# A fused layernorm, filter and FFN kernel: the first tiles centred on VectorE and scaled on ScalarE, the first up blocks by halves of the tokens, and chunk 1's rows loaded and their statistics taken sooner

## The reference, cut to what matters

```python
x = L0_attn_x                        # (2, 4096, 256) float32: 8192 tokens of 256
xn = (x - mean(x)) / sqrt(var(x) + 1e-5)          # over the last axis
# branch 1: a circulant filter whose spectrum hangs on one number D, got by
# counting how many of the first 4, 16, ... 1024 values of xn lie above their mean
x1 = ifft(fft(xn) * filt(D)).real
bits = (sigmoid(x1 @ W_el + b_el) > 0.5)          # 24 a token, then a code word is mended
branch1 = x1 + corrected(bits) @ W_le + b_le
# branch 2: FFN, 256 -> 1024 -> 256
h = gelu(xn @ w1 + b1)
branch2 = h @ w2 + b2
out = x + branch1 + branch2
```

## Time and profile before

| | |
|---|---|
| median of 3 runs | 407.75 us (407.51 to 407.8) |
| the profiled execution | 407.3 us, of which the span of the profile is 405.5 us |
| PE busy | 99% of the span, 1774 matmuls |
| DVE, ACT, POOL busy | 74%, 55%, 21% |

### The profile page before, as it was taken

One profiled execution on the slowest core, in us unless ns is written; L12 is line 12 of the kernel. 1 busy time (PEld: TensorE's weight loads), 2 busy tenths in 40 slices (PEclk: granted clock), 3 DMA queues, 4 the chain that ended last, 5 costly groups with the idle time before them and its releaser, 6 DMA issues.

```text
span 405.5 us, 5548 instructions
## 1 busy us (share of the span) xinstructions
PE 400.7 (99%) x1774; PEld 329.1 (81%) x1774; DVE 298.7 (74%) x512; ACT 223.3 (55%) x333; POOL 87.2 (21%) x102
## 2 busy tenths in 40 slices
PE   8999999999999999999999999999999999999997
PEld 3888888888888888888888888888888888888886
DVE  5879985878658795677957788476974868757656
ACT  3967556557354664537545474554736556365561
POOL 3142421313003131121313013131121312113000
PEclk9999999999999999999999999999999999999999
DMA  6554333213333213333123332023333031111011
GB/s 187 218 158 156 104 103 106 63 42 104 103 104 98 44 65 103 104 103 97 46 64 104 103 104 90 26 91 103 104 103 78 40 89 53 54 52 52 2 52 52
DMA packets 15307, 35.75 MB, mean 88 GB/s; under 512 B 5440, under 2 KB 6592, under 8 KB 15296
## 3 DMA queue, kind: packets, MB, share of 16 engines
q1 hardware_dynamic: 15152, 35.49, 27.4%
q10 hardware_dynamic: 144, 0.13, 0.1%
HBM read 27.17 MB, written 8.45 MB: 88 GB/s over the span
## 4 chain that ended last, share of the span: by engine, by line
PE 97%; DMA 1%; DVE 1%; POOL 0%; SPq 0%; issue 0%
PE p_h L964 43%; PE p_f L982 28%; PE p_f L987 14%; PE p_s L1030 5%; PE p_l L1017 4%; PE p_s L1038 2%; DMA x_sb<-x 1%; PE p_f L997 0%; SPq L248 0%; DVE stats L830 0%; POOL row_nums L361 0%; DVE rows_sb L817 0%; PE p_g L1006 0%; PE p_l L1006 0%; PE p_s L1139 0%
## 5 line engine op out<-in xcount | busy, mean ns | idle before, releaser
L446 ACT ACTIVATE h<-p_h,small_sb 128x512 f32<-128x512 f32 x128 | 88.2, 689 | 139.4 <-PE p_h L964 138.9
L633 DVE TENSOR_TENSOR h_lo<-h,h_hi 128x512 fp32r<-128x512 f32 x128 | 102.9, 804 | 69.2 <-ACT h_hi L454 69.2
L982 PE MATMUL p_f<-h_hi,w_hi 128*128 128x512 f32 x252 | 98.3, 390 | 0.0
L982 PE MATMUL p_f<-h_hi,w_lo 128*128 128x512 f32 x252 | 98.1, 389 | 0.0
L369 POOL TENSOR_TENSOR uv<-xn 128x512 f32<-128x512 f32 x30 | 59.3, 1996 | 126.0 <-DVE xn L618 126.0
L454 ACT CAST h_hi<-h 128x512 fp32r<-128x512 f32 x128 | 79.5, 621 | 5.8
L964 PE MATMUL p_h<-xT_hi,w_hi 128*128 128x512 f32 (+1 forms) x258 | 79.4, 389 | 0.0
L964 PE MATMUL p_h<-xT_lo,w_hi 128*128 128x512 f32 (+1 forms) x258 | 79.2, 388 | 0.0
L964 PE MATMUL p_h<-xT_hi,w_lo 128*128 128x512 f32 (+1 forms) x258 | 79.0, 387 | 0.0
L987 PE MATMUL p_f<-h_lo,w_hi 128*128 128x512 f32 x252 | 77.6, 389 | 0.0
L964 PEld LDWEIGHTS p_h<-xT_lo,w_hi 128*128 128x128 f32 x258 | 48.3, 188 | 10.3 <-DVE xT_lo L839 0.2
(11 more groups left out here) (127 smaller groups left out, 325.2 us busy)
## 6 DMA issues: line engine op xcount, KB each, us to landing
xt_sb<-xt SPq DMA_DIRECT2D x16, 512.0 KB, 5.3
x_sb<-x SPq DMA_DIRECT2D x15, 512.0 KB, 4.6
rows_sb<-rows_dram SPq DMA_DIRECT2D x15, 512.0 KB, 4.4
out<-xt_sb SPq DMA_DIRECT2D x15, 512.0 KB, 2.8
xt_sb<-w SPq DMA_DIRECT2D x3, 512.0 KB, 7.5
xt_sb<-w SPq DMA_DIRECT2D x2, 256.0 KB, 4.5
x_sb<-x SPq DMA_DIRECT2D x2, 128.0 KB, 2.1
x_sb<-x SPq DMA_DIRECT2D x1, 256.0 KB, 3.2
```

The source lines that it names most:

```text
L446: nc.scalar.activation(h[m % 2][:], p_h[:, m % 2, :], ACT.Gelu, bias=small_sb[:, S_B1 + m:S_B1 + m + 1]).then_inc(gelu_done, 1)
L633: nc.vector.tensor_tensor(h_lo[m % HR][:], h[m % 2][:], h_hi[m % HR][:].bitcast(F32), ALU.subtract).then_inc(h_lo_done, 1)
L982: mm(p_f[:, a, :], w[:, m, a * HF:(a + 1) * HF], h_hi[r][:], start=(m == 0 and w is w2_hi), stop=False, skip_group_check=True)
```

## The change

- Chunk 0's first two tiles: DVE subtracts the mean as soon as it is known (`centred0`), ACT multiplies with the inverse deviation (`scaled0`). The other two tiles stay with one DVE instruction each, now behind the first `w1_lo` piece.
- The identity matrix is made on POOL (`affine_select` on the matrix of ones, in front of four memsets) and is no longer loaded.
- `w1`'s first quarter becomes two eighths, in loads and in splitting.
- Up blocks 0 and 1 are made together (`first_ups`): hi by hi of the first 256 tokens of both, then the transposes of the second tiles, then the rest by halves. Both finish at the end of this stretch; `up(0, 0, 2)` follows.
- ACT does gelu of block 1 in front of the first `w2` piece.
- SP loads `small` first, and chunk 1's rows in front of the first half of `w2`. DVE takes their statistics in front of `hidden_lo(0, 0)`.
- The third tiny sum (`logged`) stands behind `down(0, 2)` and no longer behind `down(0, 1)`.

The diff, cut to its core:

```diff
-W1_PARTS = ((0, 2), (2, 4), (4, 6), (6, MB))
-W1_LOADS = ((0, 2), (2, 4), (4, MB))
+W1_PARTS = ((0, 1), (1, 2), (2, 4), (4, 6), (6, MB))
+W1_LOADS = ((0, 1), (1, 2), (2, 4), (4, MB))
@@ SP
-            sp.dma_start(id_sb[:], ident).then_inc(id_in, 16)
+            sp.dma_start(small_sb[:], small).then_inc(small_in, 16)
             load_w1(0)
-            sp.dma_start(small_sb[:], small).then_inc(small_in, 16)
             load_w1(1)
+            load_w1(2)
             sp.dma_start(con[:], consts).then_inc(con_in, 16)
+            load_x(1)
             load_w2(0)
-            load_x(1)
-            load_w1(2)
+            load_w1(3)
             load_w2(1)
@@ POOL
+            pool.wait_ge(pool_set, 3)
+
+            nc.gpsimd.affine_select(out=id_sb[:], in_=ones[:], pattern=[[1, P]], base=0, channel_multiplier=-1,
+                                    compare_op=ALU.is_equal, fill=0.0).then_inc(id_made, 1)
             for q in range(2):
                 nc.gpsimd.memset(cw[q][:].bitcast(F32), 0.0).then_inc(cw_set, 1)
                 nc.gpsimd.memset(le2[q][:].bitcast(F32), 0.0).then_inc(le_set, 1)
-            pool.wait_ge(pool_set, 3)
@@ ACT
+            act.wait_ge(rstd_done, 1)
+            for j in range(HALF):
+                act.wait_ge(centred0, j + 1)
+                nc.scalar.mul(xn0[:, j, :], xn0[:, j, :], row_nums[0][:, 1, j:j + 1]).then_inc(scaled0, 1)
             w1_part_hi(0)
+            w1_part_hi(1)
             for g in range(2):
                 act.wait_ge(t0_done, g + 1)
                 nc.scalar.copy(half_tokens(xT_hi[0], g), half_bank(g)).then_inc(t0_hi, 1)
-            w1_part_hi(1)
+            w1_part_hi(2)
             act.wait_ge(small_in, 16)
             gelu(0, 0, first=True)
             hidden_hi(0, 0, first=True)
+            gelu(0, 1, first=True)
             w2_part_hi(0)
-            gelu(0, 1, first=True)
             hidden_hi(0, 1, first=True)
@@ DVE
             aggregate(0, range(HALF))
+
+            dve.wait_ge(stat_done, 1)
+            for j in range(HALF):
+                nc.vector.tensor_scalar(xn0[:, j, :], x_sb[0][:, j, :], mv[0][:, j, 0:1], None,
+                                        ALU.subtract).then_inc(centred0, 1)
...
-            for g in range(2):
-                normalise(g)
             w1_part_lo(0)
+            dve.wait_ge(rstd_done, 2)
+            for j in range(HALF, CT):
+                nc.vector.tensor_scalar(xn0[:, j, :], x_sb[0][:, j, :], mv[0][:, j, 0:1], row_nums[0][:, 1, j:j + 1],
+                                        ALU.subtract, ALU.mult).then_inc(xn0_done, 1)
...
             nc.vector.tensor_reduce(fr_s[:, 0, :], fr_a[:], AX.X, ALU.add).then_inc(part_sums, 1)
+            statistics(1, 1)
+            dve.wait_ge(stats_made, 3)
+            aggregate(1)
             hidden_lo(0, 0)
...
             hidden_lo(0, 1)
-            statistics(1, 1)
-            dve.wait_ge(stats_made, 3)
-            aggregate(1)
             hidden_lo(0, 2)
@@ PE
+            def first_ups():
+
+                turn_rows(0, scaled0)
+                pe.wait_ge(t0_hi, 1)
+                for m in range(2):
+                    pe.wait_ge(w1_hi_ready, m + 1)
+                    half_up(m, 0, (0,))
+                turn_rows(1, xn0_done)
+                pe.wait_ge(w1_ready, 1)
+                half_up(0, 0, (1,))
+                pe.wait_ge(t0_lo, 1)
+                half_up(0, 0, (2,))
+                half_up(1, 0, (2,), last_term=1)
+                pe.wait_ge(w1_ready, 2)
+                half_up(1, 0, (1,), last_term=1)
+                pe.wait_ge(t0_hi, 2)
+                half_up(0, 1, (0, 1))
+                half_up(1, 1, (0, 1))
+                pe.wait_ge(t0_lo, 2)
+                half_up(0, 1, (2,)).then_inc(up_done, 1)
+                half_up(1, 1, (2,)).then_inc(up_done, 1)
...
-            for m in range(LOOK):
+            first_ups()
+            for m in range(2, LOOK):
                 up(0, 0, m, first=True)
...
-                if m == 1:
+                if m == 2:
                     summed_over(16, 1, fr_d[:, 0:1], logged, dim_made)
```

More of the change, by code:

```diff
@@ L62, with build @@
 S_END = S_WEL + KB * LAT
-def build(nc, x, xt, small, latent, w1, w2, ident, consts, basis, out):
+def build(nc, x, xt, small, latent, w1, w2, consts, basis, out):
     ctx = ExitStack()
@@ L176, in build @@
         w2_in = [sem(f"w2_in{i}") for i in range(len(W2_LOADS))]
-        id_in, con_in, basis_in, small_in = sem("id_in"), sem("con_in"), sem("basis_in"), sem("small_in")
+        id_made, con_in, basis_in, small_in = sem("id_made"), sem("con_in"), sem("basis_in"), sem("small_in")
         latent_in, stored = sem("latent_in"), sem("stored")
@@ L190, in build @@
         veps_done, rstd_done, mean_done = sem("veps_done"), sem("rstd_done"), sem("mean_done")
[L191 removed]
+        centred0, scaled0, xn0_done, t0_done, t0_hi, t0_lo = sem("centred0"), sem("scaled0"), sem("xn0_done"), sem("t0_done"), sem("t0_hi"), sem("t0_lo")
         fr_taken, xc0_made = sem("fr_taken"), sem("xc0_made")
@@ L522, in _ @@
             hidden_hi(0, 0, first=True)
+            gelu(0, 1, first=True)
             w2_part_hi(0)
-            gelu(0, 1, first=True)
             hidden_hi(0, 1, first=True)
-            w1_part_hi(2)
+            w1_part_hi(3)
             gelu(0, 2, first=True)
@@ L529, in _ @@
             w2_part_hi(1)
-            w1_part_hi(3)
+            w1_part_hi(4)
             gelu(0, 3, first=True)
@@ L811, in w2_part_lo @@
                                         ALU.subtract).then_inc(w2_ready, 1)
[L813 to L819, removed]
             for j in range(HALF):
@@ L840, in _ @@
                                         ALU.subtract).then_inc(t0_lo, 1)
+                if g == 0:
+                    w1_part_lo(1)
             table = [P, NS, FRE]
@@ L847, in _ @@
             values = fr_v[:, :].unsqueeze(1).broadcast_to(table)
-            w1_part_lo(1)
+            w1_part_lo(2)
             first_rows = p_s[:, :, :].rearrange("p g (a t) -> p (g a) t", t=P)[:, :, 0]
@@ L862, in _ @@
             nc.vector.tensor_reduce(fr_s[:, 2, :], fr_a[:], AX.X, ALU.add).then_inc(part_counts, 1)
-            w1_part_lo(2)
+            w1_part_lo(3)
             hidden_lo(0, 1)
-            statistics(1, 1)
-            dve.wait_ge(stats_made, 3)
-            aggregate(1)
             hidden_lo(0, 2)
@@ L874, in _ @@
                                     ALU.add).then_inc(logged, 1)
-            w1_part_lo(3)
+            w1_part_lo(4)
             w2_part_lo(1)
@@ L945, in up @@
                     if first and m == m0:
[L947 to L966, removed]
@@ L967, in up @@
-                last.then_inc(up_done, 1)
+                        pe.wait_ge(w1_ready, n + 1)
+                pe.wait_ge(gelu_done, MB * c + m - 1)
+                n = 0
+                for w, xp in ((w1_hi, xT_hi), (w1_lo, xT_hi), (w1_hi, xT_lo)):
+                    for k in range(KB):
+                        last = mm(p_h[:, m % 2, :], w[:, k, m * P:(m + 1) * P], xp[par][:, k, :],
+                                  start=(n == 0), stop=(n == 3 * KB - 1))
+                        n += 1
@@ new lines, in up, with turn_rows, half_up @@
+                last.then_inc(up_done, 1)
+            def turn_rows(g, ready):
+                for j in range(HALF):
+                    pe.wait_ge(ready, j + 1)
+                    for k in range(KB):
+                        last = nc.tensor.transpose(half_bank(g)[:, k, j * P:(j + 1) * P],
+                                                   xn0[:, g * HALF + j, k * P:(k + 1) * P], id_sb[:])
+                last.then_inc(t0_done, 1)
+            def half_up(m, g, terms, last_term=2):
+                tok = slice(g * GTOK, (g + 1) * GTOK)
+                for n in terms:
+                    w, xp = ((w1_hi, xT_hi), (w1_lo, xT_hi), (w1_hi, xT_lo))[n]
+                    for k in range(KB):
+                        last = mm(p_h[:, m, tok], w[:, k, m * P:(m + 1) * P], xp[0][:, k, tok],
+                                  start=(n == 0 and k == 0), stop=(n == last_term and k == KB - 1), skip_group_check=True)
+                return last
@@ L1132, in _ @@
                 mm(p_f[:, 0, :], idle[:, 0:P], idle[:], start=True, stop=True)
[L1133 to L1141, removed]
+            pe.wait_ge(id_made, 1)
             pe.wait_ge(pool_set, 3)
-            for m in range(LOOK):
+            first_ups()
+            for m in range(2, LOOK):
                 up(0, 0, m, first=True)
@@ L1219, in constants @@
     assert a.sum(axis=1).min() >= 4
-    return np.eye(P, dtype=f4), con, basis
+    return con, basis
 def layouts(inputs):
@@ L1255 @@
     arrays = {name: np.ascontiguousarray(a) for name, a in layouts(inputs).items()}
-    for name, a in zip(("ident", "consts", "basis"), constants()):
+    for name, a in zip(("consts", "basis"), constants()):
         arrays[name] = a
```

## The result

The changed kernel is slower: 409.58 us median of 6 runs (409.27 to 409.65) against 407.59 (407.06 to 407.8), ratio 1.0048, 95% interval 1.0035 to 1.0061. The forecast was 408.15 us and no difference; the time lies outside its range (407.4 to 409.1).

What follows compares the result with a forecast made beforehand. PE was taken to bound the kernel, with only the first 12 us to win from. 0.47 (up block 2) plus 0.05 (circulant), taken as 0.45, gave 408.15 us, no difference; range 407.4 to 409.1.

Steps and rivals of the forecast that it cites:

- The new wait for block 0's gelu: In front of up block 2: blocks 0 and 1 complete together, gelu is uncovered and PE stands 0.85 us.
- The first down block: PE arrives at about 15.0 us; `w2_lo` is ready at 14.5, so no cost was taken.
- The identity: Made on POOL at about 1.2 us: 0.5 to 1.0 us long, up to 2.1 us hidden, no cost.
- The sooner statistics: Chunk 1's statistics on DVE, sooner by 2.5 us: PE waits for none of it, worth nothing.
- where I summed 0.47: End of the head: up block 2 starts at 12.15 rather than 11.68 us, 0.47 us later.
- my 7.8 to 8.1: Head: sign of being right, PE's first half matmul starts at 7.8 to 8.1 us.
- my 6.3 to 6.5: Head: the first transposes start at 6.3 to 6.5 us, behind PE's zeros, rather than 6.66.
- my 12.15: Start of up block 2 in us, behind block 0's gelu; bounds 12.0 to 12.5.
- ACT's two multiplications: Head, scaled tiles: at 0.43 us each, begun after the inverse deviation at 5.13, they end at about 5.95.
- The step that failed: Filter chain to D: third sum late, POOL's chain still 5.3 us, ending at 28.4; PE waits 0.05 us at the circulant.
- one number decides: Head: PE is dense from up block 2 on, so only that block's start matters; at most 1.7 us to win.
- a wait at the circulant: Rival: the later chain to D makes PE wait 0.5 us there, 408.6 us; chance 0.10.

Runs made afterwards that it cites:

- sum_back: The changed kernel with the third small sum (logged) again behind the second down block: 407.89 us, ratio 1.0012 to the kernel before.
- stats_back: The changed kernel with chunk 1's statistics again behind the second `hidden_lo` on DVE, the third sum still late: 409.72 us, ratio 1.0053.
- centre_waits: The changed kernel with DVE waiting for POOL's `filt_w` before centre of chunk 1, the sum still late: 409.31 us, ratio 1.0045.
- both probes: The kernel before plus two DVE subtractions (two SBUF inputs) or four `bn_stats` (one input) behind the sixth `hidden_lo`: 409.68 and 410.7 us, one run each.
- before_two_inputs: The kernel before plus two DVE subtractions of 128x1024 (two SBUF inputs) behind the sixth `hidden_lo`: 409.68 us, run once, only its trace read.

## Why the prediction was wrong

**Right.** That PE bounds the kernel, and that a change counts only where it makes PE wait. The new wait for block 0's gelu is there, 0.69 us where I had 0.85, and its mechanism was shown: with block 0 finished first it is 0.22. The first down block had no wait. The identity cost 0.29 us on POOL and nothing in time (`var_eps` at 4.15 in both). The sooner statistics were worth nothing by themselves. `angle` ended at 22.96 (23.1).

**The head: about right, though the changed kernel's own trace was lucky.** Up block 2 started 0.19 us later, where I summed 0.47. From PE's first half matmul it took 4.26 us (4.20 in the sum; the half matmuls came 0.119 apart, 0.117 in the sum), but that matmul came at 7.61, before my 7.8 to 8.1, and the transposes at 6.00, before my 6.3 to 6.5. In this execution the zeros were over early: twelve matmuls in 4.71 us, where they took 5.30 in the kernel before. Three more executions with the same list in the head, sum_back, stats_back and centre_waits, start up block 2 at 12.31, 12.13 and 12.65; the four lie around my 12.15. Two smaller terms were off: ACT's two multiplications ended at 6.26 and not at 5.95, and the inverse deviation came at 5.31 and not at 5.13, for a reason that belongs to the next paragraph.

**The step that failed** is this one: "POOL's chain took 5.3 us (20.91 to 26.20): 28.4 ... Before, 0.6 us was to spare ..., now nothing: 0 to 0.3 us, I take 0.05." With it falls the sentence that one number decides, the start of up block 2. The late sum and its place were right, and a wait at the circulant was among the rivals with 0.5 us. Its size was wrong because I moved the chain in time and kept its length. The chain isn't 5.3 us of work; it is what its neighbour on DVE makes of it. It took 7.28 us, `filt_w` was there at 30.24 and not at 28.4, and PE waited 1.57 us. The single edit makes 1.0042 on the kernel before, and undoing it brings 1.0048 down to 1.0012. The warning stood in the trace before: POOL's first chain instruction, on four columns, takes 1.11 us there too and ends 0.05 us behind DVE's 128x1024 subtraction, and I didn't look at which instructions of the chain were long and why. The same cause made the inverse deviation late: the new centring on DVE stood beside `var_eps`, which took 0.35 us rather than 0.20.

Two terms beside it were off as well, and neither made the miss. The circulant's first product needs only the first half of `basis_w`: PE started 0.56 us behind `filt_w` (30.24, 30.80), where I charged 0.7 to 0.8. So the slack before was some 0.8 us and not 0.6, and a chain of 5.3 us would have cost nothing: ended at 28.25, it lets PE start at 28.81, and PE was free for the circulant at 29.07 (the last pair in front starts at 28.61, and the next instruction follows such a pair by 0.46). And chunk 1's statistics came 4.2 us sooner (13.01 rather than 17.24), not 2.5; my own times, 13.2 against about 17.2, already gave 4.0.

**The sum again, with what was measured:** 0.19 for block 2; 0.10 more until the first down block, of which 0.08 lies in the first pair behind the new wait; 1.57 for the wait at the circulant and 0.16 for the matmuls in front of it, whose ends the next instruction would otherwise have overlapped; 0.17 for the circulant itself, whose four matmuls take 0.53 us to the next start rather than 0.36. That is 2.19, and at the end of the span 2.1 are left.

What stays open is the head's own size. What moved its start from run to run can be read in part: in centre_waits the split of `w1`'s second eighth waited for its landing until 7.45, and in sum_back the first four transposes took 1.05 us, where they took 0.75 in the changed kernel. So I can't say more than that all of the change but the late sum is 0 to 0.3% slower (1.0012, interval 0.9998 to 1.0027).

## What to carry to other kernels

When a chain of small instructions is moved, its length doesn't move with it: lay the neighbour engine's list of the new place beside it, and look first for the instructions of the chain that are longer than their shape explains. A consumer that has 0.8 us to spare is a resource; count what every reordering takes from it, also where the consumer stands late in the program, as the circulant does. And two accumulations that finish together have no work left to cover the first one's evacuation: finish one bank, then fill the other.

## What the runs showed of the hardware

A POOL `tensor_tensor` of 2 to 16 columns (other than the power, 0.7 to 1.0 us) takes 0.20 us at best, which it has while DVE reads one SBUF operand by `bn_stats`. It takes up to 1.21 us (stats_back), until the running DVE instruction ends, while DVE reads two SBUF operands (128x1024, 1.22 us). The Trainium skill, GPSIMD Engine Reference, Key points, says that the engine shares its SBUF interfaces with VectorE, with contention when DVE instructions have two SBUF inputs or use a mode with two ports. The traces of both probes agree, and they put a size on it: it isn't a share of bandwidth, the small instruction lasts as long as the rest of the large one (it ends 0.05 to 0.06 us behind it).

One SBUF input isn't always harmless. In the changed kernel `var_eps` started under a DVE `tensor_scalar` with one input and ended 0.05 us behind it:

```profile
4.10 0.35 DVE L830 TENSOR_SCALAR rows_sb<-x_sb,mv 128x256 f32<-128x256 f32 x1
4.15 0.35 POOL L359 TENSOR_TENSOR var_eps<-mv,eps 128x2 f32<-128x2 f32 x1 [1.71 <-DVE mv L604]
```

It did so in each of the six kernels with this centring. But in before_two_inputs a `var_eps` at 5.79 took its 0.20 us under the `tensor_scalar` that normalises, begun at 5.73. No run says what sets these cases apart, or the first from `bn_stats`.

Beside POOL's small instructions DVE doesn't pay: its 128x1024 subtractions of centre and scale are 1.20 to 1.23 us in every run. Beside a long one it does. In the kernel before, a `hidden_lo` that starts under POOL's `uv` (128x512, two inputs) takes 1.78 us and ends 0.55 us behind it:

```profile
74.08 2.35 POOL L369 TENSOR_TENSOR uv<-xn 128x512 f32<-128x512 f32 x1
75.20 1.78 DVE L633 TENSOR_TENSOR h_lo<-h,h_hi 128x512 fp32r<-128x512 f32 x1
```

That holds for 15 of its 128, with 0.89 to 1.78 us; the 15 that start in front of a `uv` take 0.68, the 98 that meet none 0.64 to 0.70. So which engine starts first matters here too.

The diagonal by `affine_select` (128x128) took 0.29 us as the first instruction of its kind and started at 1.13, 0.07 us behind the memset in front of it, so the trace shows no load of code there.
